# Routing a mixture of experts in two groups of two batches, in half tiles of 128 rows

## What is computed

```python
x = _L0_conv_ref(x, theta_w, phi_w, proj_w)     # softmax(theta^T phi / 8) applied to x, projected, plus x
t = _to_tokens(x)                                # 4 x 1024 tokens of 128
t = t + _L1_attn_ref(_ln_t(t), Wk, bk, Wq, bq, Wv, bv)
t = t + _L1_ffn_ref(_ln_t(t), Wg, bg, W1, b1, W2, b2)

def _L1_ffn_ref(x, Wg, bg, W1, b1, W2, b2):
    gate_logits = xf @ Wg + bg
    top_w, top_i = jax.lax.top_k(gate_logits, 2)
    top_w = jax.nn.softmax(top_w, axis=-1)
    for e in range(8):                           # 128 -> 512 -> 128
        h = jax.nn.gelu(xf @ W1[e] + b1[e], approximate=False)
        out = out + w_dense[:, e:e + 1] * (h @ W2[e] + b2[e])
```

## Time and profile before

| | |
|---|---|
| median of three runs | 542.87 us (540.98 to 543.97) |
| the profiled execution's own time | 542.02 us |
| its span, first to last instruction | 540.1 us |
| mean granted clock of TensorE | 0.885 |
| TensorE matmuls busy | 397.8 us (74%) |
| VectorE busy | 403.1 us (75%) |
| ScalarE busy | 291.1 us (54%) |
| GpSimd busy | 339.8 us (63%) |

### The profile page before, as it was taken

The page is one execution under the profiler, slowest core; times in us unless marked ns, Lnnn a source line. Parts: engine busy times, 40 slices in busy tenths (PEclk is TensorE's granted clock), DMA queues, the critical chain, the costliest instruction groups (busy, mean ns, idle before and its releaser), DMA issues.

```text
span 540.1 us, 13443 instructions
## 1 busy us (share of the span) xinstructions
PE 397.8 (74%) x3902; PEld 294.2 (54%) x3903; DVE 403.1 (75%) x1119; ACT 291.1 (54%) x567; POOL 339.8 (63%) x361
## 2 busy tenths in 40 slices
PE   3767689999797998999884483001989898989336
PEld 2433356666575665666654362000778797979212
DVE  2578979988886878898878766700688898989457
ACT  3537887887675997776663123200545455555102
POOL 8000336567997558887599777773087878778800
PEclk9878999999998999999997597555899999999855
DMA  5730004200000000000620111332223323232176
GB/s 195 182 54 1 0 1 94 66 3 1 1 0 2 1 2 1 2 1 1 140 77 10 55 51 51 89 94 59 51 75 85 85 83 88 77 91 76 44 249 227
DMA packets 44244, 33.30 MB, mean 62 GB/s; under 512 B 17702, under 2 KB 37161, under 8 KB 44201
## 3 DMA queue, kind: packets, MB, share of 16 engines
q1 hardware_dynamic: 39594, 23.24, 17.1%
q0 software_dynamic: 4608, 9.51, 5.3%
HBM read 18.98 MB, written 13.73 MB: 61 GB/s over the span
## 4 chain that ended last, share of the span: by engine, by line
POOL 27%; PE 25%; DVE 20%; issue 17%; ACT 6%; DMA 3%; POOLq 0%; ACTq 0%; SPq 0%; DVEq 0%
POOL zbuf L503 12%; POOL ybuf L606 9%; PE PV L618 7%; PE SC L618 7%; PE MX L618 6%; DVE mx L1303 5%; PE PR L618 4%; DVE EL L1326 4%; POOL EL L544 2%; ACT EH L1032 2%; DVE TOK L1579 2%; ACT QK L950 2%; DVE QK L1271 1%; POOL carry L604 1%; DVE TOK L1584 1%
## 5 line engine op out<-in xcount | busy, mean ns | idle before, releaser
L544 POOL TENSOR_TENSOR EL<-E,EH 128x1024 f32 (+1 forms) x31 | 67.0, 2160 | 58.2 <-ACT EH L1032 58.2
L1031 ACT ACTIVATE E<-SC 128x512 f32<-128x512 f32 x128 | 77.2, 603 | 48.0 <-PE SC L618 34.1
L618 PE MATMUL PV<-VH,EH 128*128 128x129 f16 x512 | 97.2, 227 | 2.4 <-DVE TOK L1346 1.9
L606 POOL DMA_INDIRECT ybuf<-QK,yid x80 | 87.1, 1089 | 18.3 <-issue 12.5
L618 PE MATMUL SC<-QK 128*128 128x512 f16 x320 | 90.5, 386 | 9.9 <-ACT EH L1032 7.2
L618 PE MATMUL PV<-VH,EL 128*128 128x129 f16 x512 | 96.8, 224 | 0.0
L618 PE MATMUL PV<-VL,EH 128*128 128x128 f16 x512 | 96.7, 222 | 0.0
L1303 DVE TENSOR_REDUCE mx<-MX 128x1 f32<-128x1024 f32 x64 | 78.0, 1218 | 20.2 <-PE MX L618 19.9
L1032 ACT ACTIVATE EH<-SC 128x512 f32 (+1 forms) x128 | 77.5, 605 | 0.0
L503 POOL DMA_INDIRECT zbuf<-ZZ,posi x64 | 65.4, 1022 | 18.9 <-issue 18.9
L618 PE MATMUL MX<-EL,EH 128*128 x640 | 59.4, 246 | 1.6 <-DVE QK L1536 1.6
(11 more groups left out here) (200 smaller groups left out, 860.4 us busy)
## 6 DMA issues: line engine op xcount, KB each, us to landing
EH<-zbuf SPq DMA_DIRECT2D x40, 130.0 KB, 2.2
X<-in_x_dram SPq DMA_DIRECT2D x4, 512.0 KB, 5.1
zbuf<-zer SPq DMA_DIRECT2D x16, 128.0 KB, 3.3
X<-in_L_ffn_W_dram SPq DMA_DIRECT2D x1, 2048.0 KB
EL<-ybuf SPq DMA_DIRECT2D x4, 512.0 KB, 5.6
EH<-ybuf SPq DMA_DIRECT2D x4, 512.0 KB, 8.9
out_dram<-X SPq DMA_DIRECT2D x8, 256.0 KB, 2.7
ybuf<-QK,yid POOLq DMA_INDIRECT x80, 2.3
```

The lines of the kernel that those rows point to most:

```text
L544: nc.gpsimd.tensor_tensor(EL[:, w % 2, ds(i * 2, 2), c], E32h[1], EH[:, w % 2, ds(i * 2, 2), c], ALU.subtract).then_inc(e32_free[1], 1)
L606: nc.gpsimd.indirect_dma_start(out=ybuf, out_offset=bass.IndirectOffsetOnAxis(ap=yid[:, b, q:q + 1], axis=0), in_=y32[:, b, q, :], in_offs ...
L618: return nc.tensor.matmul(o, w, r, start=start, stop=stop)
L1031: nc.scalar.activation(E32h[h][:, p, :], SC[:, p, :], ACT.Exp, scale=sc)
```

## The change

1. **Two groups.** Batches 0 and 1 are group 0, batches 2 and 3 group 1. Each has its own lists in `zbuf`, its own table (`tile_table(g)`), its own pads (`pads(g)`) and its own semaphore for scatters. The table of group 0 is made behind the placing of batch 1, in the last unit's step. SyncE loads the tiles of group 0 when that group's 32 scatters have landed; between the two groups' tiles stand the pads of group 1.
2. **Half tiles.** A tile (of 40, 20 for each group) is two half tiles of 128 rows (`TR = P`), each with its own expert. A load is two DMAs with an address each, and every matmul of the loop has 128 moving columns: 24 in `hidden`, 26 in `output`. TensorE loads 16 and 4 experts into registers where it loaded 8 and 2.
3. **Bias by matmul.** The expert bias b2 is in `B2`, of which rows 0 and 32 hold its high and low part and the others zero; a matmul with ones opens every output. High and low products add up in the same PSUM columns, so VectorE has one output operation. `B2` is made in the step of unit 0 by ScalarE and VectorE.
4. **Work moved in the loop.** ScalarE makes the whole of hh. `carry` and its operation are gone. A `tin` buffer is free when its tile's output is made (`y_ready`), and there are 20 output buffers in place of 8. The programs of SyncE, GpSimd, ScalarE and VectorE are written out for all tiles.
5. **Combining early.** Before tile 30, SyncE waits for group 0's outputs to land and reads them back; in tiles 32 to 39 VectorE mixes two token tiles each, those of group 0. The rest follows the loop.
6. **Last unit.** GpSimd scatters two tiles per pair instead of one. Three EL halves (pairs 0 to 2 of unit 7) move from GpSimd to VectorE (`e_low_late`).

TensorE, in the expert loop: the start of one tile's hidden product. Before, then after; PV is one of two PSUM buffers for it, EH holds the transposed rows.

The diff, cut to its core:

```diff
+G = 2
+GB = B // G
+TR = P
+DR = 2 * TR
+CAP = GB * S + TR
+SPAN = E * CAP + E * TR
+NH = GB * S * 2 // TR + E
+ND = NH // 2
+NT = G * ND
+Y_BUFS = ND
+MIX = 10
...
+            def pads(g):
+                sp.wait_ge(table_ready, 3 * g + 1)
+                for e in range(E):
+                    low = g * SPAN + e * CAP
+                    r = sp.value_load(padrow[0:1, g, e:e + 1], min_val=low, max_val=low + GB * S)
+                    pad = zbuf[ds(r, TR), :]
+                    sp.dma_start(pad[:, 0:2 * P], zer[:, 0, :]).then_inc(pad_done[g], 16)
+                    sp.dma_start(pad[:, 2 * P:ROW], padid[:, 2 * g * E + e, :].bitcast(F16)).then_inc(pad_done[g], 16)
+            def load_tile(j):
+                b = j % IN_BUFS
+                if j >= IN_BUFS:
+                    sp.wait_ge(y_ready, j - IN_BUFS + 1)
+                for q in range(2):
+                    n = 2 * j + q
+                    r = sp.value_load(tabi[0:1, 0, n:n + 1], min_val=0, max_val=G * SPAN // TR - 1)
+                    sp.dma_start(tin[:, b, q], zbuf[ds(r * TR, TR), :]).then_inc(tin_full[b], 16)
...
+            sp.wait_ge(pad_static, 16 * 2 * G)
+            for g in range(G):
+                pads(g)
+                sp.wait_ge(pad_done[g], 16 * 2 * E)
+                sp.wait_ge(table_ready, 3 * (g + 1))
+                sp.wait_ge(scattered[g], 16 * 2 * T * GB)
+                for j in range(ND * g, ND * (g + 1)):
+                    if j == ND + MIX:
+                        for b in range(Y_BUFS):
+                            sp.wait_ge(y_out[b], 32)
+                        for k in range(2 * GB):
+                            load_outputs(k)
+                    load_tile(j)
+            for b in range(Y_BUFS):
+                sp.wait_ge(y_out[b], 32 * G)
+            for k in range(2 * GB, 2 * B):
+                load_outputs(k)
+            for k in range(2 * B):
+                store(k)
...
+                    late = late_pair(u, a, i)
+                    if late is not None and not (isinstance(late[1], int) and late[0] == UNITS - 1):
+                        e_low(*late)
...
-                        scatter(i)
-            for t in range(PAIRS, TT):
+                        scatter(2 * i)
+                        scatter(2 * i + 1)
...
             def hidden(j, b, first):
+                for q in range(2):
+                    e = expert(pe, tile_expert, 2 * b + q)
+                    r = slice(q * TR, (q + 1) * TR)
+                    for c in range(HC):
+                        o_ = WIDE[b % 2][:, c * DR + q * TR:c * DR + (q + 1) * TR]
+                        w = ds(e * HID + c * P, P)
+                        mm(o_, W1H[:, w], zT[:, b % 2, 0, r], True, False)
+                        mm(o_, W1H[:, w], zT[:, b % 2, 1, r], False, False)
+                        last = mm(o_, W1L[:, w], zT[:, b % 2, 0, r], False, True)
...
             def output(j, b, first, carried_over=False):
                 for q in range(2):
+                    e = expert(pe, last_experts if carried_over else tile_expert, 2 * (b % 2 if carried_over else b) + q)
+                    o_ = MX[:, (b % 2) * HALF + q * P:(b % 2) * HALF + (q + 1) * P]
+                    mm(o_, ones16[:], B2[:, ds(e * P, P)], True, False)
                     for c in range(HC):
+                        k = slice(c * DR + q * TR, c * DR + (q + 1) * TR)
                         g = ds(e * HC + c, 1)
+                        mm(o_, hh[:, b % 2, k], W2HL[:, g, 0, :], False, False)
+                        mm(o_, hh[:, b % 2, k], W2HL[:, g, 1, :], False, False)
+                        last = mm(o_, hl[:, b % 2, k], W2HL[:, g, 0, :], False, c == HC - 1)
...
-            pe.wait_ge(table_ready, 3)
+            pe.wait_ge(table_ready, 3 * G)
...
+                act.wait_ge(b2_in, 32)
+                for r in (0, 32):
+                    cp(B2[r:r + 1, :], B232[r:r + 1, :], WS).then_inc(b2_high, 1)
...
+                cp(hh[:, b, :], h32[:, b, :]).then_inc(hh_ready, 1)
...
+                    if u == UNITS - 1 and i > 0:
+                        e_low_late(u, i - 1)
...
+                words = tin[:, j % IN_BUFS, :, 2 * P:ROW].bitcast(I32)
+                for q in range(2):
+                    n = 2 * j + q
+                    nc.vector.scalar_tensor_tensor(out=yid[:, b, q:q + 1], in0=words[:, q, 1:2],
+                                                   scalar=tabf[:, 1, n:n + 1], in1=words[:, q, 0:1],
+                                                   op0=ALU.not_equal, op1=ALU.add).then_inc(yid_ready, 1)
                 dve.wait_ge(y_full, j + 1)
+                dve.wait_ge(yid_ready, 2 * (j + 1))
+                sums = MX[:, (j % 2) * HALF:(j % 2) * HALF + DR].rearrange("p (q d) -> p q d", q=2)
+                nc.vector.tensor_scalar(y32[:, b], sums, 1 / WS, None, ALU.mult).then_inc(y_ready, 1)
...
+            rows_T(0)
+            rows_T(1)
+            for j in range(NT):
+                low_halves(j)
+                if j + 2 < NT:
+                    rows_T(j + 2)
                 if j >= 2:
+                    output(j - 2)
+                k = j - (ND + MIX + 2)
+                if 0 <= k < T * GB // 2:
+                    mixes(range(4 * k, 4 * k + 4))
             for j in (NT - 2, NT - 1):
+                output(j)
+            for k in range(T * GB // 2, T * B // 2):
+                mixes(range(4 * k, 4 * k + 4))
```

More of the change, by code:

```diff
@@ L429, in _ @@
[L429 to L440, removed]
@@ L597, in _, with put @@
                 scatter(t)
-            def put(j4, b):
-                pool.wait_ge(y_ready, j4 + (b + 1))
-                pool.wait_ge(carried, j4 + (b + 1))
-                nc.gpsimd.tensor_tensor(carry[:, 0:1], carry[:, 1:2], carry[:, 1:2], ALU.add).then_inc(carried, 1)
+            def put(j):
+                b = j % Y_BUFS
+                pool.wait_ge(y_ready, j + 1)
                 for q in range(2):
@@ L608, in put @@
                         in_=y32[:, b, q, :], in_offset=None).then_inc(y_out[b], 16)
-            with pool.Fori(0, NT // IN_BUFS) as i:
-                for b in range(IN_BUFS):
-                    put(i * IN_BUFS, b)
+            for j in range(NT):
+                put(j)
         @block.tensor
@@ L859, in hidden @@
             def hidden(j, b, first):
-                e = expert(pe, tile_expert, b)
                 pe.wait_ge(zt_ready, j + 1)
@@ new lines, in mix @@
+            def mix(n):
+                t, half = divmod(n, 2)
+                if half == 0:
+                    if t % PAIRS == 0:
+                        dve.wait_ge(y_in[t // PAIRS], 16)
+                    src, w = yin[t // T][:, t % T, 0, :], WT[:, 0, t:t + 1]
+                else:
+                    src, w = yin[t // T][:, t % T, 1, :], WT[:, 1, t:t + 1]
+                    dve.wait_ge(mixed, t + 1)
+                nc.vector.scalar_tensor_tensor(out=TOK[:, t, :], in0=src, scalar=w, in1=TOK[:, t, :], op0=ALU.mult,
+                                               op1=ALU.add).then_inc(summed if half else mixed, 1)
@@ new lines, in mixes @@
+            def mixes(ns):
+                tiles_ = sorted(set(n // 2 for n in ns))
+                for half in range(2):
+                    for t in tiles_:
+                        mix(2 * t + half)
+            rows_T(0)
+            rows_T(1)
+            for j in range(NT):
+                low_halves(j)
+                if j + 2 < NT:
+                    rows_T(j + 2)
+                if j >= 2:
+                    output(j - 2)
+                k = j - (ND + MIX + 2)
+                if 0 <= k < T * GB // 2:
+                    mixes(range(4 * k, 4 * k + 4))
```

298 lines of the change are left out of this document (108 added, 190 removed).

## The result

Four runs of the changed kernel took 590.36 us in the median (587.79 to 591.61), four of the kernel before beside them 542.88: a ratio of 1.087, with an interval of 1.083 to 1.092. The forecast was 523 us, 510 to 535: wrong, and on the wrong side of the kernel before. The profiled run spans 588.3 us, 66.8 more than the 521.5 of the forecast's sum.

What follows compares the result with a forecast made beforehand. It took the first hole, the loop's chain of TensorE matmuls and the tail as bounds. Terms 3.0 - 1.3 - 26.4 + 9.2 + 10.1 + 3 - 0.8 - 13.7, the first two inside -26.4, gave -18.6: 523 us, range 510 to 535.

Steps and rivals of the forecast that it cites:

- The step that failed: TensorE's expert loop: 54 matmuls of 128 columns at 57 ns, 3.08 us a tile, +0.23 a tile, +9.2 us.
- the weight load sets the pace: Rival, expert loop: 98 ns weight loads show at 128 columns, 5.3 us a tile, 611 us, slower; chance 0.07.
- First hole: Before the expert loop: TensorE waits for tables and W2's low halves, starting at 349.4 instead of 375.78, -26.4 us.
- the bias itself: Start of the run: ScalarE and VectorE make the bias operand, one partition costing what 128 do, +3.0 us.
- The last unit: Unit before the loop: EL moved to VectorE -2.2, ranking -2.7, group 0's table +3.6; together -1.3 us.
- the -2.2 for VectorE's EL: Last unit: three EL given to VectorE mostly fit its waits for ScalarE, four pairs taking 22.9 us.
- the ranking: Behind the last unit's pairs: small VectorE steps delayed less by GpSimd's EL, -2.7 us.
- SyncE between the groups: Mid-loop: group 1's pads delay tile 20, TensorE stalls +7.6 us, then some matmuls at half clock, +2.5.
- +3 for the mixes: Last eight tiles of the loop: VectorE's four mixes on top make 3.3 us a tile with waits, +3 us.
- The tail: From last matmul to end: half the mixes already done in the loop, 21.0 us instead of 34.7, -13.7.

Runs made afterwards that it cites:

- e8: Changed kernel with TensorE's expert constant (no register instructions), VectorE copying next rows before low halves, group 1's pads after 8 loads: 511.78 us, 0.944 of the kernel before.
- e18: Changed kernel with one register address per half tile for all four chunks, wrong chunks multiplied: 527.16 us, 0.973 of the kernel before.
- e7: Changed kernel with the first half tile's expert used for both halves, 19 register instructions a tile instead of 38: 529.37 us, 0.974 of the kernel before.

## Why the prediction was wrong

**The step that failed** is "The attention has exactly this shape, a new weight per 128 columns and as many register steps between: 24 in 1.37 us, 57 ns each. 54 x 57 = 3.08". The 57 ns is a true figure of the weight load and the matmul (e8, e18). It is not a rate at which such instructions with their register steps can be supplied. The attention's 24 come behind matmuls of 512 columns, as the timeline of the kernel before shows just ahead of the earlier trace rows:

```profile
244.20 0.81 PE L618 MATMUL SC<-QK 128*128 128x512 f16 x3
244.85 0.59 PE L618 MATMUL MX<-QK 128*128 128x512 f16 x2
245.28 0.22 PE L618 MATMUL PV<-VH,EH 128*128 128x129 f16 x1
```

While those run, the next instructions are stored up; the burst then draws on them. The register instructions in the same trace, 16 for these 24 matmuls, keep a slower pace: an ISA of theirs comes at 245.098, 245.335 and 245.572 us, one every 0.237 us for three matmuls, 79 ns a matmul. That is the pace of the changed loop's hidden, and the first of them came before the matmuls of 512 columns had ended.

The earlier trace rows is, besides, the first pass of the attention's loop, right behind two passes that are written out and have no register instructions at all. Other passes of the same trace show the price, at the granted clock of 1.00. The first pair of rows is from a written-out pass, the second from a pass of the loop; each is the first of the 24 and the matmul behind them:

```profile
206.86 0.22 PE L618 MATMUL PV<-VH,EH 128*128 128x129 f16 x1
...
208.23 0.81 PE L618 MATMUL SC<-QK 128*128 128x512 f16 x3
...
215.98 0.22 PE L618 MATMUL PV<-VH,EH 128*128 128x129 f16 x1
...
217.55 0.82 PE L618 MATMUL SC<-QK 128*128 128x512 f16 x3
```

1.37 us against 1.57. Between 183 and 230 us all four written-out groups take 1.37 and all eight of the loop 1.53 to 1.96, although wide matmuls run shortly before each. So the trace that the forecast was made from already held the price.

In the changed loop every matmul is narrow and there is next to nothing to draw on. Term: +9.2 forecast, about +79 measured (4.83 - 2.86 = 1.97 a tile).

**The rival "the weight load sets the pace"** (0.07) had the sign and the deciding point, a pitch above 66 ns, but not the mechanism. The records of the output's weight loads average 101 ns in the changed kernel from 400 to 480 us and 100 in e8, at 98 and 56 ns a matmul. The Trainium skill (TensorE: Matmul & The Clock Gate, Back-to-back issue gap) gives some 81 ns for sustained pairs at 128 columns; I had set that aside for the trace's 57. The changed kernel's 84 in hidden look like it, but e8's 352 matmuls in 20 us, 57 ns sustained, do not: here 81 ns is no limit of weight load and matmul, and the likeness comes from 16 register instructions. Taking it would have given a better forecast, near 575, for another reason.

With most of the register instructions gone and all other code kept, e18 and e7 took 527.16 and 529.37 us, inside the stated range: the failed step is nearly all of the miss.

**First hole**, 357.9 instead of 349.4. The mechanism held: group 0's tiles were loaded from 330.98 on, tables and W2 ended last. The timeline of VectorE, against the earlier trace rows:

```profile
303.32 0.16 DVE L1276 TENSOR_TENSOR cnt<-start,ecap 128x8 f32<-128x8 f32 x1
...
351.84 4.62 DVE L1536 SCALAR_TENSOR_TENSOR EL<-X,EL 128x1024 f16<-128x1024 f32 x4
```

W2's low halves come 8.8 later than before, not 1.7. Of this 5.6 is there by the fifth row maximum of unit 1 (93.24 instead of 87.67) and stays. The chains of the two kernels are level until 39.8 us. The first 1.1 comes by 45 us, with TensorE at a granted clock of 0.68 from 40 to 50 us where it had 0.87. Then ScalarE's steps with the bias give 2.2, VectorE's, 1.22 us long, gives 1.3, and 1.0 follows behind it, with TensorE at 0.83 from 70 to 80 us instead of 1.00. So the bias itself cost about 3.5 where +3.0 was forecast, and one partition cost what 128 do. The last unit gave +3.2 instead of -1.3. Its four pairs still take 25.1 us, so the -2.2 for VectorE's EL was nothing, and the ranking was shorter by 1.1 instead of 2.7, since steps of 8 to 64 numbers were again slower in places while GpSimd worked; the table cost 3.7. That leaves 0.6 that I can't place. The last 1.4 is a start of TensorE after W2 that I had not counted.

**SyncE between the groups**, +7.6 and +2.5 forecast, 0 measured. The pads took from 433.11 to 445.87, 12.8 us for my 13.9, and the stall failed to come only because tiles of 4.83 us leave more room: in e7, with tiles near 3.05, TensorE waits 6.7 us there, and in e18 7.6. With the lower clock behind the wait e18 loses 10.2 us there, for the 10.1 forecast. The term was right for the tile it assumed.

**VectorE**, +3 for the mixes: at 4.83 us a tile it is busy 16 us of 40, and the last tiles come as close together as the others, so nothing. In e18, with tiles of 3.02 us, the last ones beside the mixes come up to 3.39 apart, as the forecast's 3.3 had it.

**The tail**, 22.4 instead of 21.0, came as forecast, and its rows answer to the earlier trace rows:

```profile
569.83 2.24 DMA ybuf<-QK,yid
...
572.15 3.98 DMA EH<-ybuf
...
576.16 8.24 DVE TOK L1579 x31
```

So the expected gain did come, 18 us before the loop and 12 behind it, and 78 us inside the loop paid for it.

## What to carry to other kernels

A pitch measured in a burst holds for that burst: ask what the queue had stored up before it, and take a sustained rate from a stretch that goes on for longer than one batch. Before making tiles smaller, count the instructions per tile that don't shrink with it, addresses computed in registers above all; they are free as long as everything supplied takes less time than the matmuls, and cost in full from there. A row that was read in one place should be looked up in others: the attention's other passes would have shown the price. And when a chain of waits passes through another engine, look up the idle time of the engine that matters before calling it a gap.

## What the runs showed that I had not expected

- While TensorE is short of instructions, the next one comes 95 ns after an ISA and 60 ns after a REGISTER_ALU, but a pair of weight load and matmul takes some 27 to 34 (the changed kernel's trace). 19 register instructions a tile are nearly hidden under 54 matmuls of 128 columns (e7), 36 are not.
- With almost none between them, weight loads and matmuls of 128 columns keep up 57 ns for 20 us and more (e8), though the loads' records are 100 ns long.
- A wait for a semaphore stores no instructions up: behind one of 1.89 us the hidden product went at the slow pace from its first triple. Slow or wide matmuls do store them up.
